# A fused attention stage: 64-query transposes, one shift product, and the engines' lists written anew

## The chip, the cores and the metric

The kernel runs on one core of a Trainium2 chip. The metric is the device time of one execution in microseconds (us). Three executions of the kernel before gave 2872.92, 2874.45 and 2874.43 us, median 2874.43. A core has four compute engines that each work through a list of their own, and wait for each other only at semaphores: PE (the matrix engine, its weight loads shown apart as PEld), DVE (vector), ACT (scalar with a table of functions) and POOL.

## The reference

The input is 16 sequences of 256 positions by 128 channels. A state-space block (phase m) comes first, then two layers of windowed attention with a gated feed-forward part (phase f), then a power-attention block (phase p), then the same two f layers again. The change touches only phase f. What it computes for one sequence, cut to the core:

```python
h = shift_token(x)                       # channels 64..127 come from the position before
q, k, v = split(h @ wqkv, 3)             # 8 heads of 64
q, k = rotary_xpos(l2norm(q) * qs, l2norm(k) * ksc)
# windows of 64: a query sees its own window and the one before, never a later key
sim = where(mask, -inf, q @ k.T * 8);  attn = softmax(sim)
x = x + (attn @ v) @ wo
h = layernorm(shift_token(x)) * lg + lb
a, g = split(h @ w1 + b1, 2)
x = x + (a * gelu(g)) @ w2 + b2
```

## The kernel before

A sequence of 256 positions is two tiles (t = 0, 1) of 128. Heads are taken in two groups of four (g = 0, 1). A step of the program has a name made of what it does and these numbers, and every engine has one list of names; the order of a list is the order of the engine's work. Three sequences are in flight at a time in phase f (`F_STAGES` says which steps belong to the sequence that is one or two behind). `F_ORDER` is the list of a full iteration; it is run once for each sequence, 64 times in all (16 sequences, 2 layers, 2 calls). `MF`, `FP` and `PF` are lists written out for the joins from m to f, f to p and p to f. Nothing sets the order at run time; each step waits for the semaphores in its `wait_ge` lines.

The steps around the change, on PE unless said otherwise:

- `s00 s10 s01 s11` (L797, L802): scores of tile t and group g. Tile 0 has keys 0 to 127, tile 1 keys 64 to 255.
- DVE `nm` (L1002) takes the maxima, ACT `p` (L901) the exponentials, DVE `rs` (L1013) the reciprocal of the sums, POOL `pn` (L1064) multiplies by it, in place in `f_p`.
- `pT<t><g><y>` (L815): four transposes, one for each head, of the probabilities of tile t for keys 128y to 128y+127. `pT000`, `pT010` are tile 0; `pT100`, `pT110` are tile 1 with the first 128 keys, and `pT101`, `pT111` with the last 128. All go through the same PSUM half; ACT `pe..0` (L908, L911) or DVE `pe..1` (L1007) copies them out.
- `o00 o10 o01 o11` (L829): probabilities times values, on tiles of 64 columns of the array. ACT `oe` (L916) copies out.
- `xT`, `qk`, `v` (L757, L767, L777) and `T` (L784): the input's transpose, the projections, and the transposes of rotated queries and keys. ACT `sq` (L872), DVE `ss`, `kn`, `qa`, `qs` (L971, L981, L988, L995) and POOL `qb` (L1056) stand between.
- `wo` (L838), DVE `z1` (L1018), `sh` (L843 to L845), ACT `hb` (L919), DVE `st mv` (L1022 to L1028), ACT `rl rv`, DVE `hn` (L1033), `hnT` (L849): output projection, residual, token shift, layer norm and its transpose. After them come ACT `he`, `w1a` (L855), ACT `g0` (gelu, L933), `w1b`, `w1c`, and `w2` (L862).

Queries 64 to 127 of tile 1 may see none of the keys 0 to 127. So `pT100` and `pT110` transpose 128 queries by 128 keys, and ACT copies out only the columns of queries 0 to 63 (W is 64).

Of the kernel before, what the change touches and what calls it, by code (L numbers as in the profile page):

```python
# [13 lines left out]
P = 128  # L14
# [50 lines left out]
class Stages:  # L65
# [13 lines left out]
    def done(self, step):  # L79
# [11 lines left out]
    "dve": "hT nm00 pe111 rs00 ss0 cl0 nm10 kn0 z1 qa0 rs10 st mv nm01 ss1 hn cl1 qs0 rs01 kn1 qa1 nm11 u1 pe101 "  # L91
        "qs1 u0 rs11 z2",
    "pe": "T11 o01 pT110 xT s00 pT111 qk0 o11 s10 wo v0 qk1 sh s01 pT000 v1 pT100 hnT s11 w1a o00 T00 w1b T01 pT101 "
        "w1c pT010 o10 T10 w2",
    "act": "p11 pe010 Te10 oe0 Te11 pe110 p00 sq0 oe1 lr0 rn0 p10 ve0 hb sq1 pe000 rl rv p01 lr1 ve1 rn1 he g0 pe100 "
        "Te00 g1 Te01",
    "pool": "pn00 pn10 qb0 pn01 qb1 pn11 zb"}
# [35 lines left out]
       for ph, stages in (("m", M_STAGES), ("f", F_STAGES), ("p", P_STAGES))}  # L133
# [45 lines left out]

FP = {  # L180
# [1401 lines left out]
```

How the kernel before makes its waits and increments, by code:

```python
        def m_pe(pe, s, i, b):  # L482
            k, g = s.rstrip("0123456789"), int("0" + s[len(s.rstrip("0123456789")):])
            if s == "xT":
                if i == 1:
                    pe.wait_ge(m_first_loaded, 16 * len(m_first))
                pe.wait_ge(*act_m.at(i, "xr"))
                pe.wait_ge(*dve_m.at(i - 1, "lo"))
                for t in range(T):
                    mm = nc.tensor.transpose(m_xT_ps[:, t * P:t * P + P], m_xr[:, t, :], ident[:])
            elif s == "xe":
                pe.wait_ge(*act_m.at(i, "xTe"))
                if i == 1:
                    pe.wait_ge(m_set, 2)
                pe.wait_ge(*dve_m.at(i - 1, "delta"))
                for c in range(EC):
                    for j in range(CONV):
                        mm = nc.tensor.matmul(m_x_ps[:, c, :], m_inc[:, j, c * P:c * P + P], m_xT[:, j:j + L],
                                              start=j == 0, stop=j == CONV - 1)
            elif s == "skip":
                if i == 1:
                    pe.wait_ge(m_last_loaded, 16 * len(m_last))
                pe.wait_ge(*act_m.at(i, "xs"))
                for c in range(EC):
                    mm = nc.tensor.matmul(m_x_ps[:, c, :], mw["skip_w"][:, c * P:c * P + P], m_xT[:, CONV - 1:],
# [1 line left out]
            elif s == "u" or s == "bc":  # L507
                if i == 1:
                    pe.wait_ge(m_last_loaded, 16 * len(m_last))
                pe.wait_ge(*act_m.at(i, "xs"))
```

## Time and profile before

| | |
|---|---|
| median of 3 executions | 2874.43 us |
| the profiled execution: its own time, and its span | 2875.4 us, 2873.6 us |
| PE busy | 2647.1 us, 92% of the span, 18868 matrix multiplications |
| PE weight loads busy | 1819.6 us, 63% |
| DVE, ACT, POOL busy | 2260.1, 2225.5, 1223.4 us |
| first phase f (720 to 1360 us): PE busy | 617.52 of 640 us |
| second phase f (2250 to 2700 us): PE busy | 433.86 of 450 us |

The profile follows one execution. A matrix multiplication of float32 by float32 stands in the trace as two instructions (two passes); a transpose of 128 by 128 as one. Matrix multiplications are pipelined, so the duration in a row (some 280 ns for 128 columns) is longer than the spacing of two that follow each other; spacing is read from the start times of neighbouring rows. A row of a timeline merges instructions of one line that follow each other and gives the start of the first.

### The profile page before, as it was taken

Reading aid. Unit: us, or ns where it says so; the run is one execution under the profiler, and the core shown is the slowest. Engines: PE = TensorE matmul, PEld = TensorE weight load, DVE = VectorE, ACT = ScalarE, POOL = GpSimd, SP = SyncE. Lnnn points to the kernel's source line nnn. Section 1 sums busy time; section 2 is a strip of 40 time slices with the busy share of each in tenths; the row PEclk is TensorE's granted clock in tenths of the full one; section 3 lists DMA queues with packets and bytes.
Section 4 is the critical chain, followed back from the end, with each engine's and each line's share of the span. In section 5 each row is a group of like instructions: output and inputs, shape, how many; then the busy total and the mean of one; then the engine's idle time right before and its main releaser. Section 6 shows DMA issues by size and latency. Waiting matters only on the chain. (4 is left out here: it accounts for less than half of the span.)

```text
span 2873.6 us, 55943 instructions
## 1 busy us (share of the span) xinstructions
PE 2647.1 (92%) x18868; PEld 1819.6 (63%) x18868; DVE 2260.1 (79%) x3798; ACT 2225.5 (77%) x6114; POOL 1223.4 (43%) x1089
## 2 busy tenths in 40 slices
PE   6888888789999999999999999997899999999997
PEld 3454445356666666666777777774566666666665
DVE  8999999976767777777689999996667777676774
ACT  5788878557777777777799999995677777777775
POOL 5776777664444444444400000001444444444442
PEclk8999999999999999999999999997999999999998
DMA  3000000000000000000000000000000000000000
GB/s 98 1 1 1 1 1 1 0 1 2 1 1 1 13 13 1 1 1 1 13 14 2 2 2 1 2 1 1 1 2 1 1 2 13 17 5 7 7 7 7
DMA packets 15672, 17.84 MB, mean 6 GB/s; under 512 B 3838, under 2 KB 12863, under 8 KB 15295
## 3 DMA queue, kind: packets, MB, share of 16 engines
q1 hardware_dynamic: 15390, 14.26, 1.7%
q8 instruction: 156, 2.56, 0.4%
q14 instruction: 126, 1.02, 0.1%
HBM read 12.16 MB, written 2.10 MB: 5 GB/s over the span
## 5 line engine op out<-in xcount | busy, mean ns | idle before, releaser
L1064 POOL TENSOR_TENSOR f_p<-f_p,f_rs 128x512 f32<-128x512 f32 (+1 forms) x256 | 321.2, 1255 | 907.4 <-DVE f_rs L1013 907.3
L901 ACT ACTIVATE f_p<-pair,f_nm 128x128 f32<-128x128 f32 (+1 forms) x1024 | 387.4, 392 | 125.2 <-DVE f_nm L1002 125.2
L679 POOL TENSOR_TENSOR m_hc<-m_h,m_c 128x512 f32<-128x512 f32 x256 | 323.4, 1284 | 154.5 <-DVE m_h L646 120.5
L1056 POOL TENSOR_TENSOR f_qb<-f_kn,f_tab 128x512 f32<-128x512 f32 x256 | 373.5, 1480 | 24.3 <-DVE f_kn L981 21.0
L646 DVE TENSOR_TENSOR_SCAN m_h<-m_a,pair 128x1024 f32<-128x1024 f32 x128 | 292.2, 2283 | 11.6 <-ACT m_a L608 1.9
L767 PE MATMUL pair<-f_wqkv,f_hT 128*128 128x512 f32 x512 | 248.7, 609 | 18.0 <-DVE f_kn L981 14.5
L608 ACT ACTIVATE m_a<-m_delta,m_A 128x255 f32<-128x255 f32 x512 | 217.3, 496 | 59.4 <-DVE m_h L646 58.8
L533 PE MATMUL bank<-m_hc,ident 128*128 128x512 f32 x512 | 248.2, 619 | 1.4 <-DVE X L655 1.3
L815 PE MATMUL pair<-ident,f_p 128*128 128x128 f32 x1536 | 244.7, 282 | 3.7 <-DVE f_pT L1007 2.4
L855 PE MATMUL bank<-f_hnT,f_w 128*128 128x256 f32 (+1 forms) x768 | 213.4, 401 | 12.5 <-ACT f_g L933 3.1
L815 PEld LDWEIGHTS pair<-ident,f_p 128*128 128x128 f32 x1536 | 170.6, 141 | 82.2 <-issue 60.0
L1002 DVE TENSOR_REDUCE f_nm<-pair 128x4 f32<-128x512 f32 (+1 forms) x256 | 208.3, 814 | 16.0 <-PE pair L802 13.6
L802 PE MATMUL pair<-f_kT,f_qT 64*128 64x128 f32 (+1 forms) x2048 | 211.1, 325 | 0.0
L901 ACT ACTIVATION_READ_ACCUMULATOR f_p<-pair,f_nm 128x1 f32 x1024 | 209.5, 205 | 0.0
L829 PEld LDWEIGHTS pair<-f_pT,f_v 128*64 128x64 f32 x3072 | 150.5, 137 | 91.5 <-issue 91.1
L971 DVE TENSOR_REDUCE f_ss<-f_sq 128x16 f32<-128x1024 f32 x128 | 155.5, 1215 | 64.3 <-ACT f_sq L872 64.3
L829 PE MATMUL pair<-f_pT,f_v 128*64 128x128 f32 (+1 forms) x3072 | 199.0, 265 | 2.0 <-DVE f_pT L1007 2.0
L1150 PE MATMUL pair<-p_kT,p_qT 128*128 128x256 f32 (+1 forms) x1024 | 193.1, 331 | 3.0 <-ACT p_a L1226 1.7
L1234 ACT ACTIVATE p_p<-p_s,p_rm 128x256 f32<-128x256 f32 (+1 forms) x512 | 192.0, 464 | 3.6 <-DVE p_rm L1302 3.2
L802 PEld LDWEIGHTS pair<-f_kT,f_qT 64*128 64x128 f32 x2048 | 148.5, 188 | 68.7 <-issue 68.7
L784 PE MATMUL bank<-ident,f_qa 128*128 128x128 f32 x1024 | 165.0, 284 | 14.3 <-DVE f_qa L995 8.0
L1219 ACT ACTIVATE p_e<-pair,p_hgT 128x256 f32<-128x256 f32 (+1 forms) x512 | 173.2, 429 | 4.8 <-PE bank L838 2.1
(181 smaller groups left out, 6159.2 us busy)
## 6 DMA issues: line engine op xcount, KB each, us to landing
f_wqkv<-in_f_wqkv SPq DMA_DIRECT2D x4, 768.0 KB, 4.0
out_x<-X SPq DMA_DIRECT2D x16, 128.0 KB, 1.8
f_w<-in_f_w SPq DMA_DIRECT2D x4, 341.0 KB, 3.3
f_wo<-in_f_wo SPq DMA_DIRECT2D x4, 256.0 KB, 2.7
sel<-in_sel SPq DMA_DIRECT2D x1, 768.0 KB
f_w<-in_f_w SPq DMA_DIRECT2D x4, 192.0 KB, 3.2
m_taps<-in_m_taps SPq DMA_DIRECT2D x1, 512.0 KB, 3.6
X<-in_x SPq DMA_DIRECT2D x1, 512.0 KB, 8.5
```

What stands on the lines that cost most here:

```text
L533: mm = nc.tensor.matmul(bank[1][:], ident[:], m_hc[:, g % 4, n].rearrange("p c l -> p (c l)"), start=g == 0 and n == 0, stop=False, skip_g ...
L608: op = nc.scalar.activation(m_a[:, g % 2, n, c, 1:L], m_delta[:, b, c, 1:L], ACT.Exp, scale=m_A[:, c, g * GN + n:g * GN + n + 1])
L646: op = nc.vector.tensor_tensor_scan(m_h[:, g % 2].rearrange(flat), m_a[:, g % 2].rearrange(flat), pair[2][:], 0.0, ALU.mult, ALU.add)
L679: op = nc.gpsimd.tensor_tensor(m_hc[:, g % 4, n], m_h[:, g % 2, n], m_c[:, g % 2, n].unsqueeze(1).broadcast_to([P, EC, L]), ALU.mult)
L767: mm = nc.tensor.matmul(half(pair[0], x), f_hT[:, t * P:t * P + P], fw["wqkv"][:, x * 512:x * 512 + 512], start=True, stop=True)
L802: mm = nc.tensor.matmul(SC[:, slot(h), k0:k1], f_qT[r, b, h // 2, t * P:t * P + P], f_kT[r, b, h // 2, k0:k1], start=False, stop=True, ski ...
L815: mm = nc.tensor.transpose(PT_PS[:, j * P:j * P + P], f_p[:, t, j, y * P:y * P + P], ident[:])
L829: mm = nc.tensor.matmul(OT_F[DH * e:DH * e + DH, c, q0:q1], f_v[:, b, y, h, :], w, start=y == 1 or t == 0, stop=y == 0, skip_group_check=True)
L855: mm = nc.tensor.matmul(bank[1][0:HR[c], e * L:e * L + L], fw["w1"][:, x * HID + c * P:x * HID + c * P + HR[c]], f_hnT[:], start=True, sto ...
L901: op = nc.scalar.activation(f_p[:, t, j, k0:k1], SC[:, j, k0:k1], ACT.Exp, bias=f_nm[:, t, j:j + 1], accum_out=f_sm[:, t, j:j + 1])
L1056: op = nc.gpsimd.tensor_tensor(f_qb[:, t, :, o].rearrange("p (x h) d -> p x h d", x=2), f_kn[:, t, :, 32 - 32 * e:64 - 32 * e].rearrange(" ...
L1064: op = nc.gpsimd.tensor_tensor(f_p[:, t, :, k0:k1], f_p[:, t, :, k0:k1], f_rs[:, t, :].unsqueeze(2).broadcast_to([P, 4, k1 - k0]), ALU.mult)
```

## The change

Three edits.

1. The transposes `pT100` and `pT110` take 64 queries in place of 128: 64 partitions of `f_p`, a 64 by 64 identity, and 64 columns of output for each head. ACT reads their output as one stretch of 256.
2. The token shift writes both tiles with one product of 128 columns; the carry of one position from tile 0 to tile 1 is then added by a second product as before.
3. The lists of phase f and its joins are in another order.

```diff
 F_ORDER = {
-    "dve": "hT nm00 pe111 rs00 ss0 cl0 nm10 kn0 z1 qa0 rs10 st mv nm01 ss1 hn cl1 qs0 rs01 kn1 qa1 nm11 u1 pe101 "
+    "dve": "hT nm00 pe111 rs00 ss0 cl0 nm10 kn0 qa0 z1 st rs10 mv nm01 ss1 hn cl1 qs0 rs01 kn1 qa1 nm11 u1 pe101 "
         "qs1 u0 rs11 z2",
-    "pe": "T11 o01 pT110 xT s00 pT111 qk0 o11 s10 wo v0 qk1 sh s01 pT000 v1 pT100 hnT s11 w1a o00 T00 w1b T01 pT101 "
+    "pe": "T11 o01 pT110 xT s00 pT111 qk0 o11 s10 v0 wo pT000 qk1 sh s01 v1 pT100 o00 hnT s11 w1a T00 w1b T01 pT101 "
         "w1c pT010 o10 T10 w2",
-    "act": "p11 pe010 Te10 oe0 Te11 pe110 p00 sq0 oe1 lr0 rn0 p10 ve0 hb sq1 pe000 rl rv p01 lr1 ve1 rn1 he g0 pe100 "
-        "Te00 g1 Te01",
-    "pool": "pn00 pn10 qb0 pn01 qb1 pn11 zb"}
+    "act": "p11 Te10 oe0 pe010 Te11 pe110 p00 sq0 oe1 lr0 rn0 p10 ve0 hb sq1 pe000 rl rv p01 ve1 lr1 rn1 he g0 Te00 "
+        "pe100 g1 Te01",
+    "pool": "pn00 qb0 pn10 pn01 qb1 zb pn11"}
...
+                n = W if t and not y else P
                 for j in range(4):
-                    mm = nc.tensor.transpose(PT_PS[:, j * P:j * P + P], f_p[:, t, j, y * P:y * P + P], ident[:])
+                    mm = nc.tensor.transpose(PT_PS[:, j * n:j * n + n], f_p[0:n, t, j, y * P:y * P + P], ident[0:n, 0:n])
...
-                nc.tensor.matmul(bank[1][:, 0:64], shift[:], zt[:, 0, 64:128], start=True, stop=True)
-                nc.tensor.matmul(bank[1][:, 64:128], shift[:], zt[:, 1, 64:128], start=True, stop=False)
-                mm = nc.tensor.matmul(bank[1][:, 64:128], carry[:], zt[:, 0, 64:128], start=False, stop=True)
+                nc.tensor.matmul(bank[1][:, 0:128], shift[:], zt[:, :, 64:128], start=True, stop=False, skip_group_check=True)
+                mm = nc.tensor.matmul(bank[1][:, 64:128], carry[:], zt[:, 0, 64:128], start=False, stop=True,
+                                      skip_group_check=True)
...
-                                              PT_PS.rearrange("p (c k) -> p c k", c=4)[:, :, 0:W], ACT.Copy)
+                                              PT_PS[:, 0:4 * W].rearrange("p (c k) -> p c k", c=4), ACT.Copy)
```

The lists `MF`, `FP` and `PF` take the same moves where they hold phase f, with the layer norms of phase p (`n..`) put elsewhere among them.

On PE, from the output projection to the layer norm's transpose, in a full iteration before (L838 `wo`, L777 `v0` and `v1`, L767 `qk1`, L843 to L845 `sh`, L797 and L802 `s01`, L815 `pT000` and then `pT100`, L849 `hnT`):

```order
L838 MATMUL bank1<-f_wo,f_oT 128x128 x8
L777 MATMUL bank0<-f_wqkv,f_hT 128x512
L767 MATMUL pair0<-f_wqkv,f_hT 128x512 x2
L843 MATMUL bank1<-f_z1,shift 128x64
L844 MATMUL bank1<-f_z1,shift 128x64
L845 MATMUL bank1<-f_z1,carry 128x64
L797 MATMUL pair1<-band,identb 128x2x128 x2
L802 MATMUL pair1<-f_kT,f_qT 128x128 x4
L815 MATMUL pair2<-ident,f_p 128x128 x4
L777 MATMUL bank0<-f_wqkv,f_hT 128x512
L815 MATMUL pair2<-ident,f_p 128x128 x4
L849 MATMUL bank1<-ident,f_hn 128x128 x2
```

The same stretch after (the file is one line shorter above L812, so L776 is `v`, L766 `qk`, L796 and L801 are `s01`; L829 is `o00`):

```order
L776 MATMUL bank0<-f_wqkv,f_hT 128x512
L838 MATMUL bank1<-f_wo,f_oT 128x128 x8
L815 MATMUL pair2<-ident,f_p 128x128 x4
L766 MATMUL pair0<-f_wqkv,f_hT 128x512 x2
L843 MATMUL bank1<-f_z1,shift 128x128
L844 MATMUL bank1<-f_z1,carry 128x64
L796 MATMUL pair1<-band,identb 128x2x128 x2
L801 MATMUL pair1<-f_kT,f_qT 128x128 x4
L776 MATMUL bank0<-f_wqkv,f_hT 128x512
L815 MATMUL pair2<-ident,f_p 128x64 x4
L829 MATMUL pair2<-f_pT0,f_v 64x128 x4
L849 MATMUL bank1<-ident,f_hn 128x128 x2
```

`pT000` has moved ahead of `qk1` and `sh`, `v0` ahead of `wo`, and `o00` now stands between `pT100` and `hnT`.

On PE right behind that, before (L855 `w1a`, L829 `o00`, L784 `T00`, L855 with 85 rows `w1b`):

```order
L797 MATMUL pair1<-band,identb 128x2x192 x2
L802 MATMUL pair1<-f_kT,f_qT 128x192 x4
L855 MATMUL bank1<-f_hnT,f_w1 128x256 x2
L829 MATMUL pair2<-f_pT0,f_v 64x128 x4
L784 MATMUL bank0<-ident,f_qa 128x128 x4
L855 MATMUL bank1<-f_hnT,f_w1 85x256 x2
```

and after (L783 is `T00`):

```order
L796 MATMUL pair1<-band,identb 128x2x192 x2
L801 MATMUL pair1<-f_kT,f_qT 128x192 x4
L855 MATMUL bank1<-f_hnT,f_w1 128x256 x2
L783 MATMUL bank0<-ident,f_qa 128x128 x4
L855 MATMUL bank1<-f_hnT,f_w1 85x256 x2
```

Only `T00` is left between `w1a` and `w1b`.

On DVE in the same iteration before (L981 `kn0`, L1018 `z1`, L988 `qa0`, L1013 `rs10`, L1022 `st`, L1026 and L1028 `mv`, L1002 `nm01`):

```order
L981 TENSOR_TENSOR f_kn<-pair0,f_rn 128x1024
L1018 TENSOR_TENSOR f_z1<-Z,bank1 128x256
L988 TENSOR_TENSOR f_qa<-f_kn,f_tab 128x1024
L1013 RECIPROCAL f_rs<-f_sm 128x4
L1022 BN_STATS f_st<-f_hb 128x6 x2
L1026 COPY carrier<-eps 128x1
L1028 BN_AGGR f_mv<-f_st 128x2 x2
```

and after:

```order
L981 TENSOR_TENSOR f_kn<-pair0,f_rn 128x1024
L988 TENSOR_TENSOR f_qa<-f_kn,f_tab 128x1024
L1018 TENSOR_TENSOR f_z1<-Z,bank1 128x256
L1022 BN_STATS f_st<-f_hb 128x6 x2
L1013 RECIPROCAL f_rs<-f_sm 128x4
L1026 COPY carrier<-eps 128x1
L1028 BN_AGGR f_mv<-f_st 128x2 x2
```

`rs10`, for which POOL's `pn10` and then PE's `pT100` wait, now stands behind `st`, which waits for the token shift.

## Rows read from the trace of the kernel before

**Rows 1.** The page: clock granted to PE, in 40 slices of the span.

```profile
PEclk8999999999999999999999999997999999999998
```

**Rows 2.** Windows of one iteration: length, then busy us of PE, PEld, DVE, ACT, POOL.

```profile
1000.22:1026.35 26.13, 25.24 (x191) 17.62 (x190) 18.35 (x35) 19.95 (x61) 11.69 (x9) 1.00 0.01 2
```

**Rows 3.** Timeline of PE in that iteration: start, length, instruction, count, idle before.

```profile
1006.15 1.88 PE L767 MATMUL pair<-f_wqkv,f_hT 128*128 128x512 f32 x4
1007.96 0.89 PE L829 MATMUL pair<-f_pT,f_v 128*64 128x128 f32 x16
...
1012.81 1.88 PE L767 MATMUL pair<-f_wqkv,f_hT 128*128 128x512 f32 x4
1014.53 0.33 PE L843 MATMUL bank<-f_z,shift 128*128 128x64 f32 x2
1014.70 0.39 PE L844 MATMUL bank<-f_z,shift 128*128 128x64 f32 x2
1014.92 0.39 PE L845 MATMUL bank<-f_z,carry 128*128 128x64 f32 x2
1015.14 0.38 PE L797 MATMUL pair<-band,identb 128*128 128x256 bf16 x2
...
1016.59 1.02 PE L777 MATMUL bank<-f_wqkv,f_hT 128*128 128x512 f32 x2
1017.53 0.63 PE L815 MATMUL pair<-ident,f_p 128*128 128x128 f32 x4
1018.95 0.44 PE L849 MATMUL bank<-ident,f_hn 128*128 128x128 f32 x2 [0.79 <-DVE f_hn L1033]
```

**Rows 4.** Timeline of PE behind it, and around `pT110`.

```profile
1020.61 1.13 PE L855 MATMUL bank<-f_hnT,f_w 128*128 128x256 f32 x4
1021.67 0.66 PE L829 MATMUL pair<-f_pT,f_v 128*64 128x128 f32 x8
1022.26 0.65 PE L784 MATMUL bank<-ident,f_qa 128*128 128x128 f32 x4
1022.75 1.03 PE L855 MATMUL bank<-f_hnT,f_w 128*85 128x256 f32 x4
...
1030.12 0.66 PE L815 MATMUL pair<-ident,f_p 128*128 128x128 f32 x4
1030.62 0.38 PE L757 MATMUL bank<-ident,Z 128*128 128x128 f32 x2
1030.83 0.38 PE L797 MATMUL pair<-band,identb 128*128 128x256 bf16 x2
```

**Rows 5.** Timeline of ACT in the same iteration.

```profile
1015.34 0.28 ACT L919 ACTIVATE f_hb<-bank 128x128 f32<-128x128 f32 x1 [1.69 <-PE bank L845]
...
1021.78 0.84 ACT L933 ACTIVATE f_g<-bank,f_b 128x256 f32<-128x256 f32 x2
...
1028.63 0.64 ACT L916 ACTIVATE f_oT<-pair 128x512 f32<-128x512 f32 x1
```

**Rows 6.** Timeline of DVE in the same iteration.

```profile
1013.92 0.17 DVE L1013 RECIPROCAL f_rs<-f_sm 128x4 f32<-128x4 f32 x1
1015.85 0.49 DVE L1022 BATCH_NORM_STATS2 f_st<-f_hb 128x6 f32<-128x128 f32 x2 [1.75 <-ACT f_hb L920]
1016.37 0.15 DVE L1026 COPY carrier<-eps 128x1 f32<-128x1 f32 x1
...
1018.30 0.59 DVE L1033 TENSOR_SCALAR f_hn<-f_hb,f_mv,f_rv 128x128 f32<-128x128 f32 x2
```

**Rows 7.** Timeline of POOL in the same iteration.

```profile
1014.18 1.47 POOL L1064 TENSOR_TENSOR f_p<-f_p,f_rs 128x768 f32<-128x768 f32 x1 [4.83 <-DVE f_rs L1013]
```

**Rows 8.** Weight loads of the whole span by shape: count, busy us, mean ns.

```profile
L815 PEld LDWEIGHTS pair<-ident,f_p 128*128 128x128 f32 x1536 | 170.6, 141 | 82.2 <-issue 60.0 <-POOL f_p L1064 0.6
...
L838 PEld LDWEIGHTS bank<-f_wo,f_oT 128*128 128x128 f32 x1024 | 119.1, 191 | 15.0 <-issue 13.9 <-ACT f_oT L916 1.1
...
L1117 PEld LDWEIGHTS bank<-ident,p_hg 16*128 16x128 f32 x64 | 8.3, 185 | 5.3 <-DVE p_hg L1254 5.3
```

107 rows, old and new, of tables (FP, MF, PF) are left out of this document.

## The prediction

> **What bounds the kernel now.** I read the clock first: PE's granted clock stands at nine or ten tenths in all slices but two, so full speed is the state to reckon in [rows 1]. Then one iteration of phase f: it lasts 26.13 us, PE is busy for 25.24 of them, the next engine, ACT, for 19.95 [rows 2]. There are 64 such iterations (24 of the L815 transposes in each, 1536 in all [rows 8]), which is 1672 of 2873.6 us. Nothing of the change lies outside them.
>
> PE is not the whole bound, though. Follow PE through one turn [rows 3, 4]. Its only long gap is the 0.79 us before `hnT` at 1018.95. That wait belongs to a chain: the token shift ends at 1015.14, ACT starts `hb` at 1015.34 [rows 5], DVE `st` at 1015.85 and `hn` at 1018.30, ending 1018.89 [rows 6], and `hnT` starts 0.06 later. From the start of `hb` to `hnT` it is 3.61 us whatever PE does meanwhile, as long as PE has less than that to do. Behind it comes a second chain: `w1a`, then the gelu of two blocks on ACT, ending at 1021.78 + 0.84 = 1022.62 [rows 5], which `w1b` (1022.75) must wait for since it overwrites their PSUM. In between PE did `o00` and `T00` and lost nothing. From `w1b` round to the shift of the next sequence PE is the bound, with small waits. So a turn is: a stretch set by PE (`w1b` to `sh`), and two holes, behind `sh` and behind `w1a`, in which work is free up to the hole's length. What a list does is choose which work lies in the holes.
>
> **The units of PE.** The shift's passes of 64 columns follow each other at 0.11 us (two of L844 from 1014.70 to 1014.92) though 64 columns stream faster than that, as the first pair shows (0.17 us from 1014.53 to 1014.70) [rows 3]: a weight load of 128 columns is the pace there. Transposes of 128 columns come at 0.105 to 0.11 us (two of L757 from 1030.62 to 1030.83) [rows 4]. A change of the array's tiles costs 0.09 us: `qk0` to `o11` takes 1.81 us (1006.15 to 1007.96), the same four passes `qk1` to `sh`, without one, 1.72 us (1012.81 to 1014.53) [rows 3]. `pT100` and `pT110` of 64 partitions are tiles of 64 rows, so each now has a change on both sides.
>
> **The pace of the 64-query transposes** is in no row. The stationary operand is still 128 columns wide (`f_p`), only the moving one (the identity) is 64. A load in a transpose is recorded with 141 ns, one of an ordinary product with 191 [rows 8]. The latter are those that pace at 0.11, so I estimate 0.06 us for a transpose's load. It is also what 64 streamed columns took in the first pair of the shift. So: 0.06 us, with ends 0.055 and 0.11. The Trainium skill, "TensorE: Matmul & The Clock Gate", section on LDWEIGHTS, says that a load takes its columns over 1.2, 107 ns for 128 of them, and that rows do not matter. That speaks against edit 1, which would then save nothing; the 141 against 191 does not agree with one time for both, so I go by the row and keep the rule's case as a rival.
> Whether such a transpose remains one pass is not in the rows either; those of 16 rows at L1117 are two (64 loads for 16 sequences of two transposes [rows 8]). The compiled program of the changed kernel has 18740 matrix multiplications, 128 fewer than 18868, which is exactly the shift's two passes times 64. So one pass.
>
> **Part by part, in us per iteration.**
> - Shift: three products are six passes, 0.61 us from 1014.53 to 1015.14 [rows 3]. Now four passes, two fewer at 0.11: -0.22. It lies on the path, ahead of `hb`.
> - `pT000` goes from behind `s01`, inside the hole before `hnT`, where it was free, to between `wo` and `qk1`, in the stretch that PE sets, and ahead of the shift: four at 0.11, +0.44. No tiles change there. `v0` and `wo` only trade places.
> - `pT110` (1030.12 to 1030.62, 0.50 us [rows 4]): four at 0.06 in place of 0.11 give -0.20, the change of tiles behind it +0.09, the first load of `xT`, no longer hidden, +0.06. Together -0.05; ends -0.25 and +0.1.
> - `o00` leaves the place between `w1a` and `w1b`. It was 0.59 us there (1021.67 to 1022.26 [rows 4]), but `w1b` can't start before the gelu, 1022.62 plus 0.06. So -0.07, not -0.59, and PE stands idle for some 0.6 us more behind `T00`. ACT's `Te00` now goes ahead of `pe100`: nothing for PE waits longer by it.
> - The hole before `hnT` now holds `s01 v1 pT100 o00`. PE could be through early, but `pT100` waits for `pn10` on POOL, and that for `rs10` on DVE, which now stands behind `st`. It was done at 1013.92, long before [rows 6, 7]. From the start of `hb`: 0.51 to `st`; 0.40 to 0.52 to `rs10` (`st` lasts 0.49, the next instruction, which needs its result, starts 0.52 later [rows 6]); 0.26 from there to `pn10` (1013.92 to 1014.18) and 1.47 for it [rows 6, 7]; 0.06 to PE; `pT100` with one change of tiles 0.38; `o00` 0.59. That is 3.67 to 3.79 against 3.61. The chain through DVE itself is 3.61 to 3.70, with `rs10` put into it. Both arrive together; I take +0.08 (ends -0.02 and +0.18). Queued behind `pT100` are `o00` and `hnT`, and with `hnT` the whole feed-forward part.
> - `z1` goes behind `qa0` on DVE, but `wo` now ends later too, and `pT000` and `qk1` (0.44 and 1.72 us) stand between it and `sh`. Hidden. On ACT `pe010` goes behind `Te10` and `oe0`, so it takes the slot that `oe0` had at 1028.63 [rows 5] and is done by 1029.27; `o01`, which needs it, starts 0.59 ahead of `pT110`'s 1030.12 [rows 4], at 1029.53. Nothing, with 0.2 us to spare. POOL's `qb0` ahead of `pn10` and `zb` ahead of `pn11` move into its idle time (11.69 us busy of 26.13 [rows 2]). ACT copies 256 elements of `pT1.0` as before: nothing.
>
> Sum: -0.22 + 0.44 - 0.05 - 0.07 + 0.08 = +0.18 us. For the 60 iterations run from the full list: +10.8 us. The joins hold the same steps with others among them; zero, give or take 3. The profiled execution took 2875.4 us, 1.0 more than the median of 2874.4; the sum gives 2886.2 for it and 2885 for the median. The ends of the terms leave +0.02 to +0.33, so 2876 to 2894 for this case.
>
> **Rivals.**
> - PE's own work sets the turn (faster). It falls by 0.22 for the shift, 0.05 at `pT110`, and 0.11 at `pT100` (0.20 less, one change of tiles more), 0.38 in all; if the turn shortens by that, 64 times, the time is 2850. For it: 25.24 busy of 26.13 [rows 2], and `o00` fits the 0.79 us before `hnT`. Against: both holes have ends that PE doesn't set, and what left one hole opens another behind `w1a`.
> - The weight load is the pace of the 64-query transposes (slower yet). Eight at 0.11 in place of 0.06 are +0.40, `pT100`'s half of them on the path since it comes last before `o00` and `hnT`; it decides from a pace of about 0.08 us on, where each group of four costs more than it did with 128 queries. 24 us more, 2909. For it: the 185 ns of the narrow L1117 loads [rows 8]. Against: those belong to two-pass products.
> - 64 partitions from partition 0 change no tiles (about even). `pT110` is then -0.20, the path through `pT100` 0.09 shorter, where DVE's chain takes over (+0.03): -0.02 in all, 2873. For it: nothing else runs in the other half of the array. Against: the tile's size is what the 0.09 went with before.
>
> **How the numbers follow.** My forecast has 0.53, PE's work 0.20, the slow load 0.15, no change of tiles 0.12. The time is 2885, its own range 2876 to 2894. 0.2% is 5.7 us, about what a measurement of this kernel can tell from no change. Slower by more than that: three quarters of the forecast (0.38) and the slow load, 0.53. Within: the rest of the forecast but a little, and most of the third rival, 0.25. Faster: PE's work and the lower edges, 0.22. For 8 in 10 the range must take in the slow load and reach part of the way to PE's work: 2855 to 2911.
>
> **What would show it.** In the profile after: the turn near 26.3 us; idle of PE before the 85-row `w1b` with the gelu (L933) as its end, 0.6 us, that was not there; PE waiting some 0.9 us before `pT100` with POOL L1064 as its end; the wait before `hnT` nearly gone; the shift's start to the score product behind it about 0.39 us; and the spacing of `pT100` and `pT110` 0.06 us with 0.09 more at each side. I am wrong if `w1b` starts right behind `T00`, if the turn is under 26.1, or if the 64-query rows are 0.11 apart.

## The result, and the profile after

| | before | after |
|---|---|---|
| median of 9 executions each | 2873.92 us (2871.89 to 2875.72) | 2882.08 us (2880.13 to 2889.63) |
| after over before | | 1.0033, 95% interval 1.0023 to 1.0044 |
| profiled execution, its span | 2875.4, 2873.6 us | 2887.7, 2885.9 us |
| PE busy | 2647.1 us | 2619.2 us |
| DVE, ACT, POOL busy | 2260.1, 2225.5, 1223.4 us | 2275.4, 2226.6, 1285.3 us |

The change makes the kernel 8.2 us slower, although PE has 27.9 us less to do. In the profiled executions, whose spans are 12.3 us apart, PE's idle time has grown by 12.3 + 27.9 = 40.2 us. The granted clock is nine tenths or more in all but four of the 40 slices (8, 8, 7 and 7), where before it was so in all but three (8, 7 and 8 in [rows 1], which the prediction counted as two). The mean over the profiled execution is 0.977 in both.

One turn of phase f (one iteration of the full list), from one `o11` to the next, as a window (length, then busy us of PE, PEld, DVE, ACT, POOL). It answers to [rows 2]: the turn is 26.26 us in place of 26.13, and PE is busy for 24.78 of it, not 25.24.

```profile
1002.97:1029.23 26.26, 24.78 (x190) 17.51 (x189) 18.63 (x34) 19.95 (x61) 12.76 (x9) 1.00 0.12 34
```

PE in that turn, from the timeline of after. It answers to [rows 3, 4]; the second shift row (L844) is the carry.

```profile
1007.81 0.60 PE L815 MATMUL pair<-ident,f_p 128*128 128x128 f32 x4
1008.25 1.88 PE L766 MATMUL pair<-f_wqkv,f_hT 128*128 128x512 f32 x4
1009.97 0.38 PE L843 MATMUL bank<-f_z,shift 128*128 128x128 f32 x2
1010.19 0.33 PE L844 MATMUL bank<-f_z,carry 128*128 128x64 f32 x2
1010.36 0.38 PE L796 MATMUL pair<-band,identb 128*128 128x256 bf16 x2
...
1013.23 0.46 PE L815 MATMUL pair<-ident,f_p 64*128 64x64 f32 x4 [0.79 <-POOL f_p L1064]
1013.62 0.66 PE L829 MATMUL pair<-f_pT,f_v 128*64 128x128 f32 x8
1014.21 0.44 PE L849 MATMUL bank<-ident,f_hn 128*128 128x128 f32 x2
1014.48 0.49 PE L796 MATMUL pair<-band,identb 128*128 128x384 bf16 x2
...
1015.75 1.13 PE L855 MATMUL bank<-f_hnT,f_w 128*128 128x256 f32 x4
...
1017.81 1.10 PE L855 MATMUL bank<-f_hnT,f_w 128*85 128x256 f32 x4 [0.49 <-ACT f_g L933]
...
1019.98 1.13 PE L855 MATMUL bank<-f_hnT,f_w 128*128 128x256 f32 x4 [0.20 <-DVE f_u L1039]
...
1025.30 0.46 PE L815 MATMUL pair<-ident,f_p 64*128 64x64 f32 x4
1025.69 0.44 PE L756 MATMUL bank<-ident,Z 128*128 128x128 f32 x2
1025.96 0.38 PE L796 MATMUL pair<-band,identb 128*128 128x256 bf16 x2
```

The brackets give PE's idle time before a row and what ended it. Before, one long wait stood before `hnT` (0.79, on DVE). Now `hnT` (1014.21) has none; the same 0.79 us stands before `pT100`, with POOL as its end, and there are two new ones, before `w1b` and before the third block `w1c`. The waits of PE over the whole span, after (us in total, times, longest; `PE pair L815 <- POOL f_p L1064` is PE's L815 waiting for POOL's L1064):

```profile
PE pair L815 <- POOL f_p L1064: 51.8, 63, 1.8
...
PE bank L855 <- ACT f_g L933: 31.4, 62, 0.9
PE bank L855 <- DVE f_u L1039: 17.4, 64, 2.2
```

and of before:

```profile
PE bank L849 <- DVE f_hn L1033: 50.9, 62, 2.6
...
PE bank L855 <- ACT f_g L933: 3.1, 4, 1.4
PE bank L855 <- DVE f_u L1039: 2.9, 4, 1.1
```

The first wait has changed its place and its releaser and kept its size (50.9, 51.8). The other two are 28.3 and 14.5 us more, 42.8 of a growth of 40.2 in all; among the smaller waits PE's wait for DVE's L995 has grown from 8.0 to 14.1 us, and others have shrunk.

ACT, DVE and POOL at the places that the prediction named, after, in answer to [rows 5 to 7]:

```profile
1010.56 0.28 ACT L919 ACTIVATE f_hb<-bank 128x128 f32<-128x128 f32 x1 [1.90 <-PE bank L844]
```

```profile
1007.59 1.23 DVE L988 TENSOR_TENSOR f_qa<-f_kn,f_tab 128x1024 f32<-128x1024 f32 x1
...
1011.07 0.49 DVE L1022 BATCH_NORM_STATS2 f_st<-f_hb 128x6 f32<-128x128 f32 x2 [1.93 <-ACT f_hb L920]
1011.47 0.16 DVE L1013 RECIPROCAL f_rs<-f_sm 128x4 f32<-128x4 f32 x1
...
1013.51 0.59 DVE L1033 TENSOR_SCALAR f_hn<-f_hb,f_mv,f_rv 128x128 f32<-128x128 f32 x2
```

```profile
1007.63 3.53 POOL L1056 TENSOR_TENSOR f_qb<-f_kn,f_tab 128x512 f32<-128x512 f32 x2 [3.28 <-DVE f_kn L981]
1011.71 1.47 POOL L1064 TENSOR_TENSOR f_p<-f_p,f_rs 128x768 f32<-128x768 f32 x1 [0.55 <-DVE f_rs L1013]
```

### The profile page after: what moved, and what is told of

Same layout as the page of the kernel before. It is cut to its first block and busy times, and to the rows that moved or that the text cites. A ratio compares the mean times of both kernels' runs of the same rounds, so it can differ in the third digit from the quotient of the medians.

```text
span 2885.9 us, 55687 instructions
## 1 busy us (share of the span) xinstructions
PE 2619.2 (91%) x18740; PEld 1814.1 (63%) x18740; DVE 2275.4 (79%) x3798; ACT 2226.6 (77%) x6114; POOL 1285.3 (45%) x1089
## 5 line engine op out<-in xcount | busy, mean ns | idle before, releaser
L1064 POOL TENSOR_TENSOR f_p<-f_p,f_rs 128x512 f32<-128x512 f32 (+1 forms) x256 | 321.0, 1254 | 642.2 <-DVE f_rs L1013 641.9
L1056 POOL TENSOR_TENSOR f_qb<-f_kn,f_tab 128x512 f32<-128x512 f32 x256 | 435.5, 1720 | 226.1 <-DVE f_kn L981 222.8
L815 PE MATMUL pair<-ident,f_p 128*128 128x128 f32 (+1 forms) x1536 | 216.8, 263 | 54.4 <-POOL f_p L1064 51.8
L855 PE MATMUL bank<-f_hnT,f_w 128*128 128x256 f32 (+1 forms) x768 | 219.0, 409 | 49.4 <-ACT f_g L933 31.4
L766 PE MATMUL pair<-f_wqkv,f_hT 128*128 128x512 f32 x512 | 246.9, 606 | 13.6 <-DVE f_kn L981 11.1
L815 PEld LDWEIGHTS pair<-ident,f_p 128*128 128x128 f32 (+1 forms) x1536 | 161.1, 140 | 132.5 <-POOL f_p L1064 103.5
L1002 DVE TENSOR_REDUCE f_nm<-pair 128x4 f32<-128x512 f32 (+1 forms) x256 | 208.2, 813 | 15.8 <-PE pair L801 13.4
L801 PE MATMUL pair<-f_kT,f_qT 64*128 64x128 f32 (+1 forms) x2048 | 211.3, 325 | 0.0
L829 PE MATMUL pair<-f_pT,f_v 128*64 128x128 f32 (+1 forms) x3072 | 199.7, 266 | 3.6 <-DVE f_pT L1007 3.1
L829 PEld LDWEIGHTS pair<-f_pT,f_v 128*64 128x64 f32 x3072 | 151.1, 138 | 76.2 <-issue 62.7
L855 PEld LDWEIGHTS bank<-f_hnT,f_w 128*128 128x128 f32 (+1 forms) x768 | 123.4, 180 | 110.5 <-ACT f_g L933 47.0
L801 PEld LDWEIGHTS pair<-f_kT,f_qT 64*128 64x128 f32 x2048 | 148.7, 188 | 68.3 <-issue 68.3
L995 DVE TENSOR_TENSOR f_qa<-f_qa,f_qb 128x1024 f32<-128x1024 f32 x128 | 173.7, 1357 | 6.6 <-POOL f_qb L1056 6.6
```

The costliest lines, as they stand in the source:

```text
L766: mm = nc.tensor.matmul(half(pair[0], x), f_hT[:, t * P:t * P + P], fw["wqkv"][:, x * 512:x * 512 + 512], start=True, stop=True)
L801: mm = nc.tensor.matmul(SC[:, slot(h), k0:k1], f_qT[r, b, h // 2, t * P:t * P + P], f_kT[r, b, h // 2, k0:k1], start=False, stop=True, ski ...
L815: mm = nc.tensor.transpose(PT_PS[:, j * n:j * n + n], f_p[0:n, t, j, y * P:y * P + P], ident[0:n, 0:n])
L829: mm = nc.tensor.matmul(OT_F[DH * e:DH * e + DH, c, q0:q1], f_v[:, b, y, h, :], w, start=y == 1 or t == 0, stop=y == 0, skip_group_check=True)
L855: mm = nc.tensor.matmul(bank[1][0:HR[c], e * L:e * L + L], fw["w1"][:, x * HID + c * P:x * HID + c * P + HR[c]], f_hnT[:], start=True, sto ...
L1056: op = nc.gpsimd.tensor_tensor(f_qb[:, t, :, o].rearrange("p (x h) d -> p x h d", x=2), f_kn[:, t, :, 32 - 32 * e:64 - 32 * e].rearrange(" ...
```

## The experiments

Eleven kernels, each timed beside the kernel before on the same chip (2874.28 us for e1 to e4, 2874.54 for e5 to e8, 2874.17 for e9 to e11). Behind a time stand the fastest and the slowest execution, behind a ratio its 95% interval. "The commonest turn" is the median distance from one `w1b` to the next in a kernel's trace, so the joins don't count in it. "Old lists" are those of before. The kernels on the old lists with both edits have their lines from L815 on one further down (L816 is the transposes, L850 `hnT`, L1034 `hn`).

**Which part costs.** Kernels e1, e2, e8 and e10 take the change apart: edits without lists, lists without edits, and the shift edit alone on either.

e1, the kernel before with edits 1 and 2 of the change and nothing of edit 3.

> The lists of before, with both edits of the instructions (64-query transposes, one shift product). My theory (a turn is a stretch of PE's work from w1b to the shift, and two holes with ends of their own): -0.22 for the shift, -0.05 at pT110, nothing at pT100, which lies in the hole before hnT. -0.27 us in 64 turns, -17 us: 2857, and the whole loss of the change is in its lists. Rival (PE's own work sets the turn): the lists move work and hardly change it, so this is as after, 2882. Rival (the narrow transposes cost by their changes of tiles): slower than the shift alone gives, above 2860.

Measured: 2859.52 us (2857.39 to 2863.64), ratio 0.9951 (0.9936 to 0.9966). As expected (2857, and a gain): the edits bring 14.8 us where the lists stay.

e2, the changed kernel with the transposes of 128 queries again:

```diff
-                n = W if t and not y else P
-                    mm = nc.tensor.transpose(PT_PS[:, j * n:j * n + n], f_p[0:n, t, j, y * P:y * P + P], ident[0:n, 0:n])
+                    mm = nc.tensor.transpose(PT_PS[:, j * P:j * P + P], f_p[:, t, j, y * P:y * P + P], ident[:])
```

> The changed kernel with 128-query transposes again, everything else as changed. My theory: pT110 gets its 0.05 back; pT100 now is on the path between pn10 and hnT, where 64 queries took 0.39 us from its start to that of o00 and 128 take 0.59 (four at 0.11 and one change of tiles), since the change of tiles ahead of it hides in the wait for POOL. +0.25 us a turn, +16: 2898. Rival (each change of tiles eats what the narrower transposes save): 2882, as after.

Measured: 2893.78 us (2892.51 to 2895.76), ratio 1.0069 (1.0054 to 1.0084). 4 us better than expected, and far from the rival (2882).

e8, the new lists and joins with neither edit of the arithmetic.

> The lists and joins of the change without its two edits of the arithmetic (128-query transposes, two shift products with their operand and sums as before). Theory (edits and lists add up: edits on old lists -14.8 against before, the 128-query transposes on new lists +11.7 against the change, the shift edit about -10 to -13 on either): lists alone +19 to +38 against before, 2893 to 2912, taken 2906. Rival (the new lists were a loss only with the edits' shorter work): near 2874 to 2885.

Measured: 2907.33 us (2902.15 to 2907.68), ratio 1.0109 (1.0093 to 1.0125), as expected (2906).

e10, on the old lists the shift edit alone.

> The lists of before, 128-query transposes, and of the change only the shift as one product for both tiles. Theory (two passes fewer at 0.11 us on the part of the turn that TensorE sets, and the chain behind the shift starts as much earlier): -0.22 us a turn, 2860.5 (2857 to 2864); so of the -14.8 of both edits on these lists the 64-query transposes give 1 to 4. Rival (the transposes give half of it, the eight shorter passes being 0.4 us a turn): 2866 to 2868.

Measured: 2860.47 us (2859.27 to 2861.01), ratio 0.9950 (0.9936 to 0.9965), as expected (2860.5).

Together, in us against the kernel before on the same chip, and in brackets the commonest turn:

| | no edit | shift | shift and 64-query transposes |
|---|---|---|---|
| old lists | 0 (26.14) | -13.7 (25.92) | -14.8 (25.87) |
| new lists | +32.8 (26.69) | +19.5 (26.47) | +8.2 (26.27) |

The shift gives 13.3 to 13.7 on either: two passes at 0.11 us, 0.22 a turn, on the path wherever it stands. The transposes give 1.1 on the old lists, which the times alone don't tell from nothing (their intervals are some 4 us to either side), and 11.3 on the new. The turns tell it: 0.05 us on the old lists, 0.20 on the new. The waits before `hnT` on the old lists, with the shift alone and then with both edits, say why:

```profile
PE bank L849 <- DVE f_hn L1033: 50.4, 62, 2.6
```

```profile
PE bank L850 <- DVE f_hn L1034: 59.9, 62, 2.6
```

The transposes of those two kernels:

```profile
L815 PE MATMUL pair<-ident,f_p 128*128 128x128 f32 x1536 | 244.7, 282 | 3.7 <-DVE f_pT L1007 2.4 <-ACT f_pT L911 0.8 <-ACT f_pT L908 0.6
```

```profile
L816 PE MATMUL pair<-ident,f_p 128*128 128x128 f32 (+1 forms) x1536 | 221.4, 266 | 3.7 <-DVE f_pT L1008 2.4 <-ACT f_pT L912 0.8 <-ACT f_pT L909 0.6
```

They are busy for 23.3 us less (half of that in the hole), and 9.5 us of it come back as a longer wait: `pT100` lies in a hole that DVE ends. In the new lists `pT100` is itself what comes late, behind POOL, and what it saves counts.

**Which step of the lists costs.** e3, the changed kernel with `pT000` behind `s01` again, in the list and where the joins have it:

```diff
-    "pe": "... s10 v0 wo pT000 qk1 sh s01 v1 pT100 o00 hnT ..."
+    "pe": "... s10 v0 wo qk1 sh s01 pT000 v1 pT100 o00 hnT ..."
```

> The changed kernel with pT000 again behind s01, in the hole before hnT, in the full list and the joins; nothing else moved. My theory: 0.44 us a turn leave the stretch that PE sets, and PE's wait of 0.79 us before pT100 takes them in; what pT100 then still waits is short. Up to -28 us, less what the later pe000 and pn10 ask: -20 to -28, 2854 to 2862. Rival (PE's work sets the turn): the same work in another place, 2882.

Measured: 2860.28 us (2858.74 to 2861.13), ratio 0.9951 (0.9934 to 0.9967): 22 us below the changed kernel, for one step of four transposes. Its waits of PE:

```profile
PE bank L855 <- ACT f_g L933: 32.9, 62, 0.9
PE pair L815 <- POOL f_p L1064: 28.0, 64, 1.3
PE bank L855 <- DVE f_u L1039: 17.4, 64, 2.2
```

`pT000` lies in the hole again, and the wait on POOL behind it shrinks from 51.8 to 28.0 us, about as much as the time falls. The waits before `w1b` and `w1c` are still there in full, and the commonest turn, 25.88 us, is that of e1 (25.87), which has neither. They cost nothing of their own. The times of e1 and e3 are alike too (2859.5 and 2860.3), but in those two further differences cancel, which the next section takes up.

e4, the changed kernel with `o00` between `w1a` and `T00` again:

```diff
-    "pe": "... pT100 o00 hnT s11 w1a T00 w1b ..."
+    "pe": "... pT100 hnT s11 w1a o00 T00 w1b ..."
```

> The changed kernel with o00 again between w1a and w1b, in the full list and the joins. My theory: both places are holes; the wait before w1b (0.49 us) goes and a wait before hnT of about 0.6 us comes, and the turn stays within 0.05 us: 2879 to 2884. Rival (o00 ahead of hnT filled a hole and gained its 0.59 us, and something else lost more): 2882 + 0.59 x 64 = 2920.

Measured: 2882.52 us (2877.41 to 2884.62), ratio 1.0026 (1.0015 to 1.0037). The same time as the changed kernel and the same commonest turn, 26.27 us, with the waits elsewhere:

```profile
PE pair L815 <- POOL f_p L1064: 53.1, 64, 1.8
PE bank L849 <- DVE f_hn L1033: 31.3, 62, 2.6
```

Before `w1b` the wait for L933 has gone (31.4 to 1.2 us) and the one before `hnT` has come (3.0 to 31.3). Where `o00` lies is worth nothing, since either hole takes it.

e11, the changed kernel with `rs10` ahead of `st` on DVE.

> The changed kernel with VectorE's two steps rs10 and st (L1013 and L1022) in their old order, so that GpSimd's scaling (L1064) for the second tile can start 0.4 to 0.5 us earlier. Theory (GpSimd's chain and VectorE's own chain to the normalised tile reach TensorE together): the wait of 0.79 us before the 64-query transposes shortens, but the same time stands before the transpose of the normalised tile then: 2882, give or take 3. Rival (GpSimd's scaling alone holds the hole open, so that the order of these two is the loss of the new lists): 60 x 0.45 = 27 less, 2855.

Measured: 2881.39 us (2878.86 to 2882.71), ratio 1.0024 (1.0014 to 1.0033). The commonest turn is 26.27 us, as without this edit. The wait on POOL falls by 34 us and the one before `hnT` rises by 26 (from 3.0), so both chains reach PE within a few tenths:

```profile
PE bank L849 <- DVE f_hn L1033: 29.2, 57, 2.6
PE pair L815 <- POOL f_p L1064: 17.7, 63, 1.3
```

**Can the hole be closed?** If a turn is PE's own stretch and two holes, more work belongs in the hole before `hnT`, or the chain that ends it must be shorter. Four kernels on the old lists with both edits try it.

e5, more work in the hole:

```diff
-    "pe": "... wo v0 qk1 sh s01 ..."
+    "pe": "... wo v0 sh qk1 s01 ..."
```

> Both edits of the arithmetic on the lists of before (2859.5 us), with one step moved on PE: the shift product ahead of the second query-and-key product instead of behind it. In the trace of the two edits on the old lists PE idles 0.94 us a turn ahead of the transpose of the normalised tile, which waits for VectorE's L1034, behind the square's sum (L972, 1.21 us), behind ScalarE's square (1.01) and copy (0.60). Theory (that hole has an end of its own, which these other steps set and not the shift product): the square is made from the moved product, so it now comes 1.7 us later for ScalarE, the chain behind it moves as well, and the turn gains nothing: 2855 to 2872, taken 2866. Rival (the shift product is what the hole waits for, so that all of the 0.94 closes): 60 x 0.94 = 56 less, near 2805; half of it, 2830.

Measured: 2874.86 us (2870.36 to 2878.81), ratio 1.0001 (0.9992 to 1.0010), 3 us beyond the upper end. The wait before `hnT` falls from 59.9 to 40.0 us, and a new one, of the score product on ACT's exponentials (L902), takes as much:

```profile
PE bank L850 <- DVE f_hn L1034: 40.0, 62, 2.6
PE pair L797 <- ACT f_p L902: 19.7, 61, 0.9
```

That would leave the time of e1, and e5 is 15 us slower than it, 0.27 us in the commonest turn (26.15). In its timeline the stretch from `v0` to the end of `sh` and `qk1` takes that much more: 0.98 us from `v0` to its successor (0.86 in e1), 0.49 for `sh` (0.39), 1.78 for `qk1` (1.72). The profile names no wait there, and no run tests why.

e6, besides that a shorter chain on ACT and DVE (`rl rv` ahead of `sq1 pe000`, `hn` ahead of `ss1`):

```diff
-    "act": "... hb sq1 pe000 rl rv p01 ..."     "dve": "... nm01 ss1 hn cl1 ..."
+    "act": "... hb rl rv sq1 pe000 p01 ..."     "dve": "... nm01 hn ss1 cl1 ..."
```

> As the run before it, and the chain from the shift product to the transpose shortened on the other two engines: on ScalarE the two small steps of the norm (L924, L927) ahead of the square and the copy, on VectorE the normalised tile (L1034) ahead of the square's sum. Theory (turn = PE's own stretch + two holes with ends of their own): the hole ahead of the transpose now closes but for what the scores and the second gate's wait take back, about 0.3 us a turn: 2842 (2835 to 2850). Rival (PE's clock and its own work are the bound already, or the square's later sum takes back what the norm gives): no gain over 2859.5.

Measured: 2918.77 us (2917.17 to 2922.74), ratio 1.0157 (1.0144 to 1.0171). The expectation is wrong by 77 us and in sign. The timelines of DVE and POOL show what it left out; the last row is the first of the two `hn` instructions by itself:

```profile
1025.12 2.50 POOL L1057 TENSOR_TENSOR f_qb<-f_kn,f_tab 128x512 f32<-128x512 f32 x2
```

```profile
1026.40 1.31 DVE L1034 TENSOR_SCALAR f_hn<-f_hb,f_mv,f_rv 128x128 f32<-128x128 f32 x1
```

In e1 it takes 0.34 us. Here it starts while POOL's second L1057 is under way (two of 1.25 us from 1025.12 end at 1027.62) and ends 0.09 after it: it stood still for 0.97 us. So it is in 61 of the 128 L1034 of e6: they overlap with a POOL instruction and take 1.30 us, the other 67 don't and take 0.34. In the rows of after above, `hn` (1013.51) starts after POOL is through (1011.71 + 1.47 = 1013.18).

e7, the shorter chain alone, PE's list as in e1.

> Both edits on the lists of before with only the ScalarE and VectorE steps moved (L924 and L927 ahead of the square and the copy, L1034 ahead of the square's sum); PE's order as it was. Theory: now ScalarE stands idle behind the shift product until VectorE has the statistics (L1023, L1029, from 1011.95 to 1012.8), with the square and its sum behind it, and the query-and-key side of the turn becomes late by the 0.9 us that ScalarE waits: slower than 2859.5 by 10 to 45, taken 2890. Rival (the hole ahead of the transpose has these two orders as its only cause): 2859.5 - 60 x 0.5 = 2830.

Measured: 2937.37 us (2931.27 to 2952.26), ratio 1.0227 (1.0199 to 1.0254). The direction is the theory's; the size is not, by 47 us. Here too `hn` stands still (its instructions take 83.0 us in all, 38.5 in e1), and PE waits for ACT's copy behind the square (L912) and for its exponentials (L902). How the loss divides between the two orders stays open; its turns are of many lengths, from 26.7 to 29.6 us.

```profile
PE pair L816 <- ACT f_pT L912: 68.9, 59, 1.2
PE pair L797 <- ACT f_p L902: 37.4, 62, 0.9
```

e9, e6 with the one swap on DVE taken back:

```diff
-    "dve": "... nm01 hn ss1 cl1 ..."
+    "dve": "... nm01 ss1 hn cl1 ..."
```

> The kernel of the second run (shift product ahead of the second query-and-key product, L924 and L927 ahead of the square on ScalarE; 2918.8 us) with one swap taken back: VectorE's L1034 stands behind the square's sum (L972) again. Theory (VectorE's L1034 can't run beside a GpSimd instruction on SBUF: in that run it took 1.30 us instead of 0.34 wherever GpSimd's L1057 was under way, and all behind it waited; behind the sum GpSimd has finished): L1034 is back at 0.34 us, the hole before the transpose of the normalised tile nearly closes, and with it the turn falls below that of the two edits on the old lists by about 0.2 us: 2847 (2838 to 2856). Rival (the order on ScalarE, which stands idle for the statistics and makes the square late, is what cost the 59 us): about as before, 2900 to 2920.

Measured: 2851.40 us (2848.26 to 2855.64), ratio 0.9919 (0.9906 to 0.9932). The group of L1034 in e6 and then in e9:

```profile
L1034 DVE TENSOR_SCALAR f_hn<-f_hb,f_mv,f_rv 128x128 f32<-128x128 f32 x128 | 94.3, 776 | 0.6 <-ACT f_rv L927 0.6
```

```profile
L1034 DVE TENSOR_SCALAR f_hn<-f_hb,f_mv,f_rv 128x128 f32<-128x128 f32 x128 | 38.4, 343 | 0.6 <-ACT f_rv L927 0.6
```

55.9 us of standing still are gone, and the kernel is 67.4 us faster for two steps in the other order. It is the fastest of all: 23 us below before, 31 below the change. Its margin is small: in its timeline `hn` starts at 1012.47, 0.10 us before the recorded end of POOL's L1057 (2.50 us from 1010.07), and takes its usual 0.59 us for two.

The hole, though, did not nearly close, which the expectation had. PE still waits 39.3 us in all before `hnT`, as in e5 (40.0). What e9 gains over e5 by `rl rv` ahead of the square is the other wait, for ACT's exponentials, which falls from 19.7 to 2.8 us.

## Why the prediction was right

The likeliest case was 2885 us, 2876 to 2894; it came out at 2882.1. In the turn the mechanism was right, term by term; that the total came so near is in part luck, as the end of this section shows. The turn taken apart, start to start, from [rows 3, 4] and the rows after (the shift that begins the next turn is a turn's length behind the first):

| stretch | before | after | difference | predicted |
|---|---|---|---|---|
| `sh` to `hnT` | 4.42 | 4.24 | -0.18 | -0.14 |
| `hnT` to `w1a` | 1.66 | 1.54 | -0.12 | 0 |
| `w1a` to `w1b` | 2.14 | 2.06 | -0.08 | -0.07 |
| `w1b` to the next `sh` | 17.91 | 18.42 | +0.51 | +0.39 |
| turn | 26.13 | 26.26 | +0.13 | +0.18 |

Point by point:
- **Shift.** 1009.97 to 1010.36 is 0.39 us, as predicted. e10 shows it on the path, 13.7 us.
- **`pT000`.** 1007.81 to 1008.25, +0.44, on the path. e3 shows it: taken back, the commonest turn is 0.39 us shorter (26.27 to 25.88) and the time 22 us. Of the 0.40 us by which the new lists lengthen the turn of both edits (25.87 to 26.27) this is nearly all.
- **`pT110`.** 0.39 us to `xT` in place of 0.50, and `xT` 0.27 in place of 0.21: -0.05, term by term. The pace is 0.06 us: four loads last 0.32 us on the PEld timeline (the row below, of `pT100`) and one 0.14, (0.32 - 0.14) / 3. So a load of 128 columns in a transpose does not pace at 0.11, and the rival on it falls. The rule that the prediction weighed from the Trainium skill ("TensorE: Matmul & The Clock Gate", LDWEIGHTS) gives 107 ns for such a load; these follow each other at 60, so the trace does not agree with it here. The prediction's own way to 0.06 was loose: 141 against 191 ns would make 0.08 of 0.11. What fits is its other reason, the 0.06 us of 64 streamed columns.
- **`o00`.** 31.4 us of waits behind `w1a` and no gain, as said. The wait is 0.49 us, not 0.6, since the row counts it from the end of `T00`; start to start the -0.07 came out as -0.08. e4 shows that the step's place is free.
- **`hb` to `hnT`.** 3.65 us against 3.69 taken (3.61 and the 0.08), and PE's wait before `pT100` 0.79 us against 0.9: 0.51 to `st`, 0.40 to `rs10` (the low end), 0.24, 1.47, 0.05, 0.39, 0.59. That both chains arrive together is what e11 shows: with `rs10` early again the turn stays as it is.
- **Missed.** Small terms of both signs. `hnT` no longer starts out of an idle PE: to the next product it takes 0.27 us (1014.21 to 1014.48), where it took 0.39 (the first of the rows of before below); -0.12. And `w1c` waits 0.20 us for DVE's L1039, whose chain goes back through ACT's second gelu to the late `w1b`: from `w1b` to `w1c` it is 2.17 us in place of 2.10 (1022.75 to the second row below). And 0.05 more lie in `w2`, which lasts 1.56 us in place of 1.50: its first product starts 0.12 us after DVE's `u0` ends, 0.26 before the change. `u0` is late by DVE's `qs1` ahead of it (L995), which takes 1.45 us in place of 1.22 since the change put POOL's `zb` beside it (the section on the hardware). That fits, and no run tests it.

```profile
1013.23 0.32 PEld L815 LDWEIGHTS pair<-ident,f_p 64*128 64x128 f32 x4 [1.61 <-POOL f_p L1064]
```

```profile
1019.34 0.48 PE L797 MATMUL pair<-band,identb 128*128 128x384 bf16 x2
...
1024.85 1.13 PE L855 MATMUL bank<-f_hnT,f_w 128*128 128x256 f32 x4
```

- **POOL at no cost.** For `qb0` ahead of `pn10` this was nearly wrong. `qb0` takes 3.53 us beside DVE's L988, which starts 0.04 before it, in place of 2.50. The prediction had it in idle time, and 0.55 us before `pn10` were left of that. For `zb` ahead of `pn11` it was wrong, as the next paragraphs show.

**Where the total was luck.** The sum was 0.18 us in each of 60 turns, 10.8, and nothing for the rest. The turn gave 0.13, which is 7.8 in 60 turns, and the time rose by 8.2. But the turns are not alike. From `w1b` to `w1b`, 41 of the 63 distances in the profiled executions are 0.11 to 0.13 us longer than before, 5.2 us together. The twelve from the 18th to the 29th (1070 to 1394 us after) lose more, eleven of them 0.6 us each, 6.9 us together. In those turns the lists of DVE and POOL hold steps of phase p's layer norm besides (`F_BESIDE` in the kernel), and PE has two waits that the other turns don't have, of 0.26 and 0.13 us. Rows of after, then of the same steps before:

```profile
1155.94 0.66 PE L783 MATMUL bank<-ident,f_qa 128*128 128x128 f32 x4 [0.26 <-DVE f_qa L995]
```

```profile
1154.22 1.67 DVE L995 TENSOR_TENSOR f_qa<-f_qa,f_qb 128x1024 f32<-128x1024 f32 x1 [0.39 <-POOL f_qb L1056]
```

```profile
1154.07 0.73 POOL L1077 TENSOR_TENSOR f_zb<-f_z,X 128x256 f32<-128x256 f32 x1
```

```profile
1183.57 1.22 DVE L995 TENSOR_TENSOR f_qa<-f_qa,f_qb 128x1024 f32<-128x1024 f32 x1 [0.21 <-POOL f_qb L1056]
```

```profile
1187.41 0.72 POOL L1077 TENSOR_TENSOR f_zb<-f_z,X 128x256 f32<-128x256 f32 x1
```

The new list has `zb` (L1077) right behind `qb1` (L1056), so it runs beside `qs1` (L995), which waits for `qb1` too and then takes 1.67 us in place of 1.22. In the old list `zb` came after `pn11`, when `qs1` was long done. In the six kernels with the new lists these twelve turns are 0.51 to 0.67 us longer than the commonest one; before, and in e1, e5, e9 and e10, they are 0.05 to 0.25 longer. That it is the place of `zb` is read from the rows, and no run moves it back.

Against that, the first `w1b` of the changed kernel stands 4.1 us earlier (622.0 us in place of 626.0), a gain of phase m and its join that the prediction had at nothing, give or take 3; its cause stays open. The last two distances are 5.1 us longer; there the granted clock is at half (1.2 GHz) in the last 17 us before, and in 33 of the last 44 us after, and the profiled execution of after is 5.6 us above the median of its kernel. So two terms taken at nothing, the twelve turns (5.4 us beyond 0.13 each) and the start (4.1), nearly cancelled. The same two stand between e3 and e1, which are 0.8 us apart in time: e3 is 5.9 us ahead at its first `w1b` and loses 5.3 from the 18th to the 29th turn.

Two slips in the prediction changed nothing. Its range of +0.02 to +0.33 us is not what the ends of its terms add up to, which is -0.12 to +0.43; the 0.13 lies in both. And it took all the change to lie inside the turns.

The rival that PE's own work sets the turn (2850) fell: PE's busy time did fall by 27.9 us, more than the 24 it said, and the turn got longer. "No change of tiles" (2873) fell with the 0.39 us of `pT110`: without a change it would be 0.50 - 0.20 = 0.30.

## What to carry to other kernels

Before pricing a moved step, cut the turn into the stretches that an engine sets and the holes that a chain on other engines ends. A step costs nearly its whole length in the first (0.39 of 0.44 us a turn here, 22 us in all) and nothing in the second, whatever the busy times say: this change took 27.9 us of work off the fullest engine and lost 8. Then look whether all turns are alike: twelve of them here, with other work beside, lost over four times as much each as the rest, and the rows of one turn don't show it. And before moving a VectorE instruction to where it could run sooner, look at what GpSimd is doing at that time; an instruction of the one can be held up by one of the other for which it waits at no semaphore.

## What the hardware showed that was not expected

Some instructions of VectorE (DVE) and GpSimd (POOL) exclude each other, so the engines wait for each other at more than the semaphores. VectorE's float32 TENSOR_SCALAR of 128 elements took 1.31 us in place of 0.34 when it began during a GpSimd TENSOR_TENSOR, and ended 0.09 us after it (e6). The other way round, GpSimd's two L1056 took 3.53 us in place of 2.50 when a VectorE TENSOR_TENSOR with both inputs in SBUF (1.23 us) had begun 0.04 us before them. VectorE's TENSOR_TENSOR waits too: L995 of after, which meets the last 0.37 us of GpSimd's L1072, takes 1.45 us, and 1.22 without it. It does not last quite to the recorded end: in e9 `hn` begins 0.10 us before GpSimd's L1057 ends and takes its 0.34 us.

```profile
1020.44 1.45 DVE L995 TENSOR_TENSOR f_qa<-f_qa,f_qb 128x1024 f32<-128x1024 f32 x1
```

```profile
1020.09 0.72 POOL L1072 TENSOR_TENSOR f_zb<-f_z,f_b 128x256 f32<-128x256 f32 x1
```

The Trainium skill has the rule ("SBUF — State Buffer", section on who interferes with whom): the pair of ports that the two share is held for the whole instruction by whoever is first, and of VectorE's instructions a `tensor_scalar` in a two-port mode and a `tensor_tensor` with two SBUF inputs want it. By that rule VectorE's reduction beside the same GpSimd work is not touched, and the traces agree: `ss1` in e1 starts in the middle of POOL's L1057 and takes its 1.21 us. So the order of before, reduction first and `hn` behind it, is the better one, as e6 against e9 shows, though the chain to `hnT` is longer by it. Below, `ss1` and POOL's L1057 in e1.

```profile
1013.27 1.21 DVE L972 TENSOR_REDUCE f_ss<-f_sq 128x16 f32<-128x1024 f32 x1
```

```profile
1011.92 2.50 POOL L1057 TENSOR_TENSOR f_qb<-f_kn,f_tab 128x512 f32<-128x512 f32 x2
```
